# Four chained recurrent layers on one core: second gate computed with the state as the stationary operand, and the update gate's first half moved

## The chip, the cores and the metric

The kernel runs on one core of a Trainium2 chip. The metric is the device time of one launch in microseconds (us). TensorE (PE) multiplies, and its weight loads (PEld) overlap its matmuls; VectorE (DVE), ScalarE (ACT) and GpSimd (POOL) do the elementwise work; SyncE (SP) issues most of the transfers.

## The reference

Everything is float32, with B = 32 sequences of T = 256 steps of D = 256 features. Four layers follow each other, each added to its input:

```python
def step0(h, t):                      # layer 0, h starts at zero
    z = sigmoid(x[t] @ W_z + h @ U_z + cond @ C_z + b_z)      # update gate
    r = sigmoid(x[t] @ W_r + h @ U_r + cond @ C_r + b_r)      # reset gate
    hh = tanh(x[t] @ W + (r * h) @ U + cond @ C + b)          # candidate
    return (1 - z) * h + z * hh
x1 = x + scan(step0)
def step1(h, t):                      # layer 1, h starts at cond
    gate = sigmoid(h @ Wh.T + x1[t] @ Wz.T + b)               # the "second gate"
    return tanh(h * (1 - alpha) + gate * x1[t])
x2 = x1 + scan(step1)
x3 = x2 + linear_recurrence(x2)       # layer 2: gates, two scans over T
out = x3 + adapter(x3, cond)          # layer 3: two products with gelu and rank-8 terms
```

The change concerns `step0` and `step1` only.

## The kernel before

**Stages.** A loop runs the two recurrences together: at step t of layer 0 it does step t - 3 of layer 1 (`LAG` = 3). After it come 16 groups of two sequences each for layers 2 and 3. Every engine has its own instruction list, written out by hand; semaphores order the engines among each other. An engine executes its list in order. TensorE's loop holds four steps to a turn (`even`, `odd`, `even`, `odd`), the loops of the other engines hold sixteen.

**Layouts.** "Features on the partitions": a state is [128, 2, 32], each half of 128 features with 32 sequences along the free axis. "By rows": four slabs of 32 partitions, in each the 32 sequences on the partitions and 64 features along the free axis. `quarter` makes 4 matmuls with a 128x32 weight block stationary and the state's 32 columns moving; its output has features on the partitions. `by_rows` makes 4 matmuls per half with the state (128x32) stationary and 64 weight columns moving; its output is by rows, and a 32x32-block transpose on VectorE turns it back. The profile has two matmul records and two weight-load records for each matmul, as the operands are float32.

**A step on TensorE.** `first_gates`: the reset gate's four quarters `reset(k, m)` (k is the half of the state that is read, m the half of the output) and the update gate's two halves `update(k)` by rows. Then `ahead_first`, input products for steps to come, which need only x; `first_cand`, four quarters on `rh_f`; `second_gate`, four quarters on `h1_f`; and at the end `second_inputs` (two steps of `x1_f` times `wz1`, every other step) or `ahead_update`. That is 24 + 16 + 16 + 16 + 16 = 88 matmuls. Waits: `reset(0, 0)` for the first half of the new state (`h_done` 1), `reset(1, 0)` for the second (`h_done` 2), `first_cand` for the two halves of `rh_f`, `second_gate` for `h1_done`.

**A step on ScalarE.** Two reset sigmoids (L391), the update sigmoid `z_rows` (L396), the tanh of layer 1 `h1_f` (L413), two candidate tanhs (L402), the second gate's sigmoid `gate_f` (L408), then copies that seed PSUM banks with constants (L361, L364, L368).

**A step on VectorE.** Two products `rh_f` (L602), the transpose of `z_rows` (L607), `x1_f` of the step before (L632), `cand_kept` = (z - 1) h (L612), two scans that make the two halves of the new state (L622); then layer 1: `gx_f` = gate x1 (L638) and for each half `h1_pre` = h1 keep1 + gx (L644, `keep1` read as a scalar per partition).

**GpSimd** adds `x2` = x1 + h1 (L288), one instruction a step, once the second gate's product is done (`gate_pre`, since that shows that `h1_f` of the step is complete).

Of the kernel before, what the change touches and what calls it, by code (L numbers as in the profile page):

```python
# [11 lines left out]
B, T, D, R = 32, 256, 256, 8  # L12
P = 128
HALVES, SLABS, BLK = 2, 4, 32
SLAB = D // SLABS
SLOT = 8
BODY = 2 * SLOT
STEPS = 2
LAG = STEPS + 1
# [11 lines left out]
def build_program(nc, io):  # L31
# [3 lines left out]
    with ctx:  # L35
        def sb(name, shape, dt=fp32):
            return ctx.enter_context(nc.sbuf_tensor(name, shape, dt))
# [4 lines left out]
        def sem(name):  # L42
            return ctx.enter_context(nc.semaphore(name))
# [13 lines left out]
        seed_z = sb("seed_z", [P, STEPS, SLAB])  # L57
        seed_g = sb("seed_g", [P, HALVES, STEPS, B])

# [8 lines left out]
        none_h = sb("none_h", [P, 2, HALVES, B, 2])  # L68
        x1_f = sb("x1_f", [P, LOOP, HALVES, B])
        gate_f = sb("gate_f", [P, HALVES, B])  # L70
        keep1 = sb("keep1", [P, HALVES, B])
        h1_f = sb("h1_f", [P, 2, HALVES, B])
        gx_f = sb("gx_f", [P, HALVES, B])
        h1_pre = sb("h1_pre", [P, 2, HALVES, B])
        x2 = sb("x2", [P, HALVES, B, T])
# [58 lines left out]
        pre_z = [rows_of(banks[4 + n]) for n in range(2)]  # L134
        pre_g = [half(banks[6 + n]) for n in range(2)]
        pre_const = banks[7][:, 128:256].rearrange("p (a m b) -> p a m b", a=2, m=HALVES)
# [21 lines left out]
            sem("zero_done"), sem("rh_done"), sem("kept_done"), sem("h_done"), sem("x1_done"))  # L158
        gx_done, pre1_done, x2_done = (
            sem("gx_done"), sem("pre1_done"), sem("x2_done"))  # L160

# [184 lines left out]
        def _(act):  # L346
# [20 lines left out]
            def seed_gate(par):  # L367
                act.activation(flat(pre_g[par]), flat(seed_g[:]), ACT.Copy).then_inc(seeded, 1)  # L368

# [35 lines left out]
            def second_gate(n, u):  # L405
                t, s = n * BODY + u, u - LAG
                act.wait_ge(gate_pre, t + 1)
                act.activation(gate_f[:], pre_g[(s // STEPS) % 2][:, :, s % STEPS, :], ACT.Sigmoid).then_inc(gate_done, 1)  # L408

# [131 lines left out]
        def _(dve):  # L541
# [14 lines left out]
            def repeated(out, *parts):  # L556
                return [bass.broadcast_tensor_aps(out, part)[1] for part in parts]

            for m in range(HALVES):
                dve.tensor_copy(seed_g[:, m], *repeated(seed_g[:, m], bias_f[:, 3, m:m + 1])).then_inc(seeds_ready, 1)  # L560
            dve.wait_ge(first_in, 16 * len(FIRST_LOADS))
# [73 lines left out]
            def second_gated(n, u):  # L635
                s = n * BODY + u - LAG
                dve.wait_ge(gate_done, s + 1)
                dve.tensor_tensor(gx_f[:], gate_f[:], x1_f[:, (u - LAG) % LOOP], ALU.mult).then_inc(gx_done, 1)  # L638

            def second_sum(n, u):  # L640
                s, at = n * BODY + u - LAG, (u - LAG) % 2
                dve.wait_ge(gx_done, s + 1)
                for m in range(HALVES):
                    new = dve.scalar_tensor_tensor(h1_pre[:, at, m], h1_f[:, 1 - at, m], keep1[:, m, 0:1], gx_f[:, m],  # L644
                                                   ALU.mult, ALU.add)
                new.then_inc(pre1_done, 1)

# [90 lines left out]
        def _(pe):  # L738
# [41 lines left out]
            def ahead_second(at, par):  # L780

                for m in range(HALVES):
                    mm = ahead(pre_g[par][:, m].rearrange("p v b -> p (v b)"), m, col(wz1),
                               lambda k: x1_f[:, at:at + STEPS, k, :])
                return mm
# [46 lines left out]
            def first_gates(u):  # L832
                par, v, now = u // STEPS, u % STEPS, (u + 1) % 2
                state = lambda k: none_h[:, now, k, :, 1]
                reset = lambda k, m, **kw: quarter(pre_rh[par][m][:, 0, v, :], w_r, state, k, m, **kw)
                update = lambda k: by_rows(pre_z[par][:, v, :], state, lambda k, j: urz[:, k, j, 1, :], (k,))
                pe.wait_ge(h_done, 1)
                reset(0, 0)
                update(0)
                pe.wait_ge(h_done, 2)  # L840
                reset(1, 0, taken=h_done).then_inc(r_pre, 1)
                reset(0, 1)
                reset(1, 1).then_inc(r_pre, 1)
                update(1).then_inc(z_pre, 1)

            def second_gate(u, sums=None):
                s = u - LAG
                gate = lambda k, m: quarter(pre_g[(s // STEPS) % 2][:, m, s % STEPS, :], col(wh1),
                                            lambda k: h1_f[:, (s - 1) % 2, k], k, m)
                pe.wait_ge(h1_done, 1)  # L850
                if sums:
                    pe.wait_ge(pre1_done, sums)
                gate(0, 0).then_inc(h1_done, -1)
                gate(0, 1)
                gate(1, 0)
                gate(1, 1).then_inc(gate_pre, 1)

# [260 lines left out]
```

## Time and profile before

| | |
|---|---|
| median of 3 runs | 979.05 us (978.9 to 980.17) |
| profiled execution | 979.33 us, span 977.5 us |
| the loop of both recurrences | up to about 602 us |
| layers 2 and 3 | the rest |
| busy share PE / PEld / DVE / ACT / POOL | 96 / 79 / 87 / 62 / 22 % |

The span is the time from the first to the last instruction of the profiled execution. Rows of the timeline give the start in us from the span's start, the duration in us, engine, line, output and inputs, and how many instructions are merged in the row (x). Idle time is in brackets with what ended it.

### The profile page before, as it was taken

The page shows a single profiled execution, that of the slowest core. Times are in us where ns is not written, and L with a number is a line of the kernel's source. Part 1 is how long each engine was busy: PE and PEld are TensorE (multiplying, and loading weights), DVE is VectorE, ACT ScalarE, POOL GpSimd, SP SyncE. Part 2 cuts the span into 40 slices and gives each one's busy share as a digit, 9 for nine tenths or more (in the row PEclk, how much of TensorE's full clock was granted, in tenths as well). Part 3 has the DMA queues.
Part 4 walks back from the last instruction along what each step waited for, and adds up shares of the span by engine and source line. Part 5 has one row for each costly group of instructions (what it writes and reads, how often), then busy time and mean ns, then how long its engine had stood idle before and what let it go on. Part 6 is the DMA issues. An engine that isn't in the chain of part 4 may idle for free.

```text
span 977.5 us, 104703 instructions
## 1 busy us (share of the span) xinstructions
PE 938.2 (96%) x46862; PEld 768.3 (79%) x46862; DVE 850.6 (87%) x2882; ACT 601.4 (62%) x2607; POOL 216.7 (22%) x430
## 2 busy tenths in 40 slices
PE   6799999999999999999999999969999999999996
PEld 6799999999999999999999997335555555555554
DVE  3588888888888888888888887799999999999993
ACT  3577767767777777777777775335455556555552
POOL 0011111111111111111111111324334334433340
PEclk7999999999999999999999999979999999999999
DMA  5031330330100101001001000100010000001001
GB/s 178 24 99 50 121 112 24 123 111 24 38 24 24 38 24 35 27 27 35 27 24 38 24 27 9 28 0 26 24 41 32 24 24 24 24 24 47 25 25 43
DMA packets 38006, 41.48 MB, mean 42 GB/s; under 512 B 5088, under 2 KB 31200, under 8 KB 36832
## 3 DMA queue, kind: packets, MB, share of 16 engines
q1 hardware_dynamic: 36832, 40.55, 13.2%
q10 hardware_dynamic: 1152, 0.66, 0.2%
q8 instruction: 11, 0.18, 0.1%
q14 instruction: 11, 0.09, 0.0%
HBM read 32.28 MB, written 8.91 MB: 42 GB/s over the span
## 4 chain that ended last, share of the span: by engine, by line
PE 61%; DVE 29%; issue 7%; DMA 2%; ACT 1%; ACTq 0%; DVEq 0%
PE bank L826 26%; PE bank L757 18%; PE bank L772 13%; DVE arena L690 11%; DVE early L709 4%; DVE early L700 4%; DVE early L713 2%; DVE early L707 2%; DVE early L688 2%; DVE early L694 2%; DMA x_ahead<-in_x 1%; PE bank L934 1%; DMA beta<-in_beta 1%; PE bank L905 1%; PE bank L951 1%
## 5 line engine op out<-in xcount | busy, mean ns | idle before, releaser
L288 POOL TENSOR_TENSOR x<-x_f,h_f 128x64 f32 x256 | 84.1, 329 | 524.9 <-PE bank L826 523.8
L934 PE MATMUL bank<-x,wl 128*128 (+1 forms) x384 | 181.3, 611 | 0.9 <-DVE rank_rows L667 0.9
L757 PE MATMUL bank<-x_ahead,early 128*32 128x64 f32 x8256 | 173.6, 221 | 3.1 <-ACT bank L361 2.2
L772 PE MATMUL bank<-early,none_h 128*32 128x64 f32 x4096 | 167.3, 223 | 3.0 <-issue 3.0
L402 ACT ACTIVATE cand_kept<-bank 128x32 f32<-128x32 f32 x512 | 99.4, 203 | 92.3 <-PE bank L826 92.3
L826 PE MATMUL bank<-none_h,early 128*32 128x32 f32 x8192 | 150.3, 196 | 3.3
L622 DVE TENSOR_TENSOR_SCAN none_h<-zero_z,cand_kept 128x64 f32<-128x64 f32 x512 | 122.6, 282 | 30.7 <-ACT cand_kept L402 3.3
L757 PEld LDWEIGHTS bank<-x_ahead,early 128*32 128x32 f32 x8256 | 142.1, 110 | 4.0 <-issue 2.3
L826 PE MATMUL bank<-h_f,early 128*32 128x32 f32 x8288 | 140.5, 203 | 4.0 <-issue 3.0
L826 PEld LDWEIGHTS bank<-none_h,early 128*32 128x32 f32 x8192 | 131.3, 111 | 13.1 <-DVE none_h L622 12.9
L826 PE MATMUL bank<-rh_f,early 128*32 128x32 f32 x8192 | 140.5, 201 | 0.9 <-issue 0.5
L934 PEld LDWEIGHTS bank<-x,wl 128*128 128x128 f32 x384 | 68.8, 191 | 88.4 <-issue 88.4
L826 PEld LDWEIGHTS bank<-h_f,early 128*32 128x32 f32 x8288 | 118.5, 110 | 5.4 <-issue 3.6
L391 ACT ACTIVATE r_f<-bank 128x32 f32<-128x32 f32 x512 | 91.2, 197 | 48.1 <-PE bank L826 29.0
L826 PEld LDWEIGHTS bank<-rh_f,early 128*32 128x32 f32 x8192 | 112.6, 111 | 3.0 <-issue 0.6
L644 DVE SCALAR_TENSOR_TENSOR h_pre<-h_f,keep,gx_f 128x32 f32<-128x32 f32 x512 | 106.3, 249 | 9.1
L456 ACT ACTIVATE arena<-bank,bl 128x512 f32<-128x512 f32 x96 | 65.9, 687 | 76.9 <-PE bank L934 76.7
L602 DVE TENSOR_TENSOR rh_f<-r_f,none_h 128x32 f32<-128x32 f32 x512 | 89.0, 192 | 23.4 <-ACT r_f L391 23.3
L690 DVE RECIPROCAL arena<-early 128x512 f32<-128x512 f32 x32 | 107.3, 3353 | 1.1
L772 PEld LDWEIGHTS bank<-early,none_h 128*32 128x32 f32 x4096 | 103.9, 112 | 3.4 <-issue 3.4
L757 PE MATMUL bank<-x_f,early 128*32 128x64 f32 x4128 | 89.1, 223 | 1.2 <-issue 1.2
L772 PE MATMUL bank<-early,x_ahead 128*32 128x64 f32 x4128 | 88.4, 222 | 0.0
(103 smaller groups left out, 1528.1 us busy)
## 6 DMA issues: line engine op xcount, KB each, us to landing
x_ahead<-in_x SPq DMA_DIRECT2D x130, 64.0 KB, 1.8
x_in<-in_x SPq DMA_DIRECT2D x32, 256.0 KB, 2.6
arena<-in_w SPq DMA_DIRECT2D x8, 1024.0 KB, 6.8
out<-y SPq DMA_DIRECT2D x32, 256.0 KB, 2.4
rank_rows<-in_bias_rows SPq DMA_DIRECT2D x1, 1024.0 KB, 6.7
arena<-scratch SPq DMA_DIRECT2D x64, 16.0 KB
early<-in_cx SPq DMA_DIRECT2D x1, 768.0 KB, 4.4
early<-in_wx SPq DMA_DIRECT2D x1, 768.0 KB, 6.5
```

Source lines behind the costliest of these rows:

```text
L288: pool.tensor_tensor(x2[:, :, :, s], x1_f[:, u % LOOP], h1_f[:, u % 2], ALU.add).then_inc(x2_done, 1)
L391: act.activation(r_f[:, m], pre_rh[par][m][:, 0, v, :], ACT.Sigmoid).then_inc(r_done, 1)
L402: act.activation(cand_kept[:, u % 2, m, :, 0], pre_rh[par][m][:, 1, v, :], ACT.Tanh, scale=-1.0).then_inc(cand_done, 1)
L456: act.activation(dst[:, unit], banks[(at + 2 * par) % 4][:], fun, bias=bl2[:, mat, unit:unit + 1]).then_inc(done, 1)
L602: dve.tensor_tensor(rh_f[:, m], r_f[:, m], none_h[:, now, m, :, 1], ALU.mult).then_inc(rh_done, 1)
L622: dve.tensor_tensor_scan(pairs(none_h, m), pairs(zero_z, m), pairs(cand_kept, m), 0.0, ALU.mult, ALU.subtract).then_inc(h_done, 1)
L644: new = dve.scalar_tensor_tensor(h1_pre[:, at, m], h1_f[:, 1 - at, m], keep1[:, m, 0:1], gx_f[:, m], ALU.mult, ALU.add)
L690: dve.reciprocal(rec[:, k], s_t).then_inc(rec_done, 1)
L757: mm = pe.matmul(out[32 * j:32 * j + 32], weights(k, j, m), moving(k), start=False, stop=False, tile_position=(0, 32 * j), skip_group_chec ...
L772: mm = pe.matmul(out[32 * j:32 * j + 32], moving(k), weights(k, j), start=False, stop=False, tile_position=(0, 32 * j), skip_group_check=True)
L826: mm = pe.matmul(out[32 * j:32 * j + 32], weights(k, j, m), moving(k), start=False, stop=k == 1, tile_position=(0, 32 * j), skip_group_che ...
L934: mm = pe.matmul(banks[(at + 2 * par) % 4][:], wl2[:, k, mat, unit], x2[:, k, bass.ds(p * GB, GB), :].rearrange("p q t -> p (q t)"), start ...
```

## The change

The second gate's product takes the same form as the update gate's. `h1_f` becomes the stationary operand and 64 columns of `wh1` move, so 8 matmuls take the place of 16; its input products (`ahead_second`) keep their number of 16 and also swap operands. The sigmoid then writes `gate_rows`, by rows, and VectorE transposes that into `gate_f`. `h1 * keep1` becomes an instruction of its own (`kept1_f`), placed between the transpose and `gx_f`, and a single addition takes the place of the two fused multiply-adds. A wait on the transpose (`gate_turned`) stands ahead of `gx_f`. In `first_gates`, `update(0)` moves from behind `reset(0, 0)` to behind `reset(1, 1)`.

```diff
             def second_gate(n, u):
-                act.activation(gate_f[:], pre_g[(s // STEPS) % 2][:, :, s % STEPS, :], ACT.Sigmoid).then_inc(gate_done, 1)
+                act.activation(gate_rows[:, s % 2], pre_g[(s // STEPS) % 2][:, s % STEPS], ACT.Sigmoid).then_inc(gate_done, 1)
...
             def second_gated(n, u):
                 dve.wait_ge(gate_done, s + 1)
+                dve.transpose(gate_f[:].rearrange("p m b -> p (m b)"), gate_rows[:, (u - LAG) % 2]
+                              ).then_inc(gate_turned, 1)
+                dve.tensor_tensor(kept1_f[:], h1_f[:, (u - LAG + 1) % 2], keep1[:], ALU.mult).then_inc(gx_done, 1)
+                dve.wait_ge(gate_turned, s + 1)
                 dve.tensor_tensor(gx_f[:], gate_f[:], x1_f[:, (u - LAG) % LOOP], ALU.mult).then_inc(gx_done, 1)
             def second_sum(n, u):
-                dve.wait_ge(gx_done, s + 1)
-                for m in range(HALVES):
-                    new = dve.scalar_tensor_tensor(h1_pre[:, at, m], h1_f[:, 1 - at, m], keep1[:, m, 0:1], gx_f[:, m],
-                                                   ALU.mult, ALU.add)
-                new.then_inc(pre1_done, 1)
+                dve.wait_ge(gx_done, 2 * (s + 1))
+                dve.tensor_tensor(h1_pre[:, at], kept1_f[:], gx_f[:], ALU.add).then_inc(pre1_done, 1)
...
             def ahead_second(at, par):
-                for m in range(HALVES):
-                    mm = ahead(pre_g[par][:, m].rearrange("p v b -> p (v b)"), m, col(wz1),
-                               lambda k: x1_f[:, at:at + STEPS, k, :])
+                for v in range(STEPS):
+                    mm = by_rows(pre_g[par][:, v, :], lambda k: x1_f[:, at + v, k, :], lambda k, j: wz1[:, k, j, :])
...
                 pe.wait_ge(h_done, 1)
                 reset(0, 0)
-                update(0)
                 pe.wait_ge(h_done, 2)
                 reset(1, 0, taken=h_done).then_inc(r_pre, 1)
                 reset(0, 1)
                 reset(1, 1).then_inc(r_pre, 1)
+                update(0)
                 update(1).then_inc(z_pre, 1)
             def second_gate(u, sums=None):
-                gate = lambda k, m: quarter(pre_g[(s // STEPS) % 2][:, m, s % STEPS, :], col(wh1),
-                                            lambda k: h1_f[:, (s - 1) % 2, k], k, m)
+                gate = lambda k: by_rows(pre_g[(s // STEPS) % 2][:, s % STEPS, :], lambda k: h1_f[:, (s - 1) % 2, k],
+                                         lambda k, j: wh1[:, k, j, :], (k,))
                 pe.wait_ge(h1_done, 1)
-                gate(0, 0).then_inc(h1_done, -1)
-                gate(0, 1)
-                gate(1, 0)
-                gate(1, 1).then_inc(gate_pre, 1)
+                gate(0).then_inc(h1_done, -1)
+                gate(1).then_inc(gate_pre, 1)
```

The seed of the second gate's banks (`seed_g`) is laid out by rows as well; its copies keep their sizes.

## Rows read from the trace of the kernel before

**Rows 1.** The page: chain that ended last, by engine; one group of instructions.

```profile
PE 61%; DVE 29%; issue 7%; DMA 2%; ACT 1%; ACTq 0%; DVEq 0%
...
L602 DVE TENSOR_TENSOR rh_f<-r_f,none_h 128x32 f32<-128x32 f32 x512 | 89.0, 192 | 23.4 <-ACT r_f L391 23.3
```

**Rows 2.** Windows, 200 to 500 us: busy time (instructions) by engine, PEclk, DMA share, GB/s.

```profile
200.00:500.00 300.00, 297.77 (x23509) 291.16 (x23501) 265.63 (x1337) 214.34 (x1204) 44.03 (x134) 1.00 0.13 36
```

**Rows 3.** The scans that make the state (L622), whole kernel.

```profile
L622 DVE TENSOR_TENSOR_SCAN none_h<-zero_z,cand_kept x512: 264/291/296, 18.3 to 601.7; 128x64 f32<-128x64 f32 x171
```

**Rows 4.** Timeline of one step, its reset gate to its new state.

```profile
304.03 0.18 PEld L826 LDWEIGHTS bank<-none_h,early 128*32 128x32 f32 x6
304.08 0.24 PE L826 MATMUL bank<-none_h,early 128*32 128x32 f32 x6
...
304.57 0.22 PE L772 MATMUL bank<-early,none_h 128*32 128x64 f32 x1
304.59 0.65 PE L757 MATMUL bank<-x_ahead,early 128*32 128x64 f32 x31
304.60 0.36 ACT L391 ACTIVATE r_f<-bank 128x32 f32<-128x32 f32 x2
304.83 0.35 DVE L602 TENSOR_TENSOR rh_f<-r_f,none_h 128x32 f32<-128x32 f32 x2
304.86 0.22 ACT L396 ACTIVATE z_rows<-bank 128x64 f32<-128x64 f32 x1
304.98 0.25 ACT L413 ACTIVATE h_f<-h_pre 128x64 f32<-128x64 f32 x1
305.08 0.44 PEld L826 LDWEIGHTS bank<-rh_f,early 128*32 128x32 f32 x32
305.08 0.55 PE L826 MATMUL bank<-rh_f,early 128*32 128x32 f32 x32
305.11 0.25 DVE L607 STREAM_TRANSPOSE zero_z<-z_rows 128x64 f32<-128x64 f32 x1
305.28 0.18 DVE L632 TENSOR_TENSOR x_f<-x_in,none_h 128x64 f32<-128x64 f32 x1
305.42 0.46 PEld L826 LDWEIGHTS bank<-h_f,early 128*32 128x32 f32 x32
305.45 0.52 PE L826 MATMUL bank<-h_f,early 128*32 128x32 f32 x31
305.47 0.23 DVE L612 SCALAR_TENSOR_TENSOR cand_kept<-zero_z,none_h 128x64 f32<-128x64 f32 x1
305.57 0.39 ACT L402 ACTIVATE cand_kept<-bank 128x32 f32<-128x32 f32 x2 [0.35 <-PE bank L826]
305.80 0.66 PE L772 MATMUL bank<-early,x_ahead 128*32 128x64 f32 x31
305.81 0.47 DVE L622 TENSOR_TENSOR_SCAN none_h<-zero_z,cand_kept 128x64 f32<-128x64 f32 x2
```

**Rows 5.** Timeline, layer 1 and the state's scans one step earlier.

```profile
303.64 0.47 DVE L622 TENSOR_TENSOR_SCAN none_h<-zero_z,cand_kept 128x64 f32<-128x64 f32 x2
303.91 0.23 ACT L408 ACTIVATE gate_f<-bank 128x64 f32<-128x64 f32 x1
304.05 0.33 POOL L288 TENSOR_TENSOR x<-x_f,h_f 128x64 f32 x1 [1.84 <-PE bank L826]
304.17 0.28 DVE L638 TENSOR_TENSOR gx_f<-gate_f,x_f 128x64 f32<-128x64 f32 x1
304.49 0.41 DVE L644 SCALAR_TENSOR_TENSOR h_pre<-h_f,keep,gx_f 128x32 f32<-128x32 f32 x2
```

**Rows 6.** Timeline at TensorE's back edge, and the scans after it.

```profile
306.51 0.16 PEld L826 LDWEIGHTS bank<-none_h,early 128*32 128x32 f32 x7 [0.21 <-DVE none_h L622]
...
308.26 0.48 DVE L622 TENSOR_TENSOR_SCAN none_h<-zero_z,cand_kept 128x64 f32<-128x64 f32 x2
```

**Rows 7.** L638 and L288 from 30 to 600 us: durations min/median/max in ns.

```profile
L638 DVE TENSOR_TENSOR gx_f<-gate_f,x_f x252: 224/284/370, 35.5 to 599.8; 128x64 f32<-128x64 f32 x126
...
L288 POOL TENSOR_TENSOR x<-x_f,h_f x251: 322/329/335, 37.9 to 599.7; 128x64 f32 x126
```

**Rows 8.** Timeline in the setup: two VectorE products, the second waiting for the first.

```profile
12.78 0.22 DVE L586 TENSOR_TENSOR scaled<-normed,gamma 128x64 f32<-128x64 f32 x1
13.04 0.22 DVE L588 TENSOR_TENSOR ada<-scaled,beta 128x64 f32<-128x64 f32 x1
```

**Rows 9.** A scan of the later stage (L700) that at times meets GpSimd work.

```profile
L700 DVE TENSOR_TENSOR_SCAN early<-early,first_one x32: 1214/1216/2292, 628.8 to 955.2; 128x514 f32<-128x514 f32 x32
```

More of the change, by code:

```diff
@@ L57, in build_program @@
         seed_z = sb("seed_z", [P, STEPS, SLAB])
-        seed_g = sb("seed_g", [P, HALVES, STEPS, B])
+        seed_g = sb("seed_g", [P, STEPS, SLAB])
         x_in = sb("x_in", [P, 2, SLOT, HALVES, B])
@@ L69, in build_program @@
         x1_f = sb("x1_f", [P, LOOP, HALVES, B])
+        gate_rows = sb("gate_rows", [P, 2, SLAB])
         gate_f = sb("gate_f", [P, HALVES, B])
@@ L73, in build_program @@
         gx_f = sb("gx_f", [P, HALVES, B])
+        kept1_f = sb("kept1_f", [P, HALVES, B])
         h1_pre = sb("h1_pre", [P, 2, HALVES, B])
@@ L134, in build_program @@
         pre_z = [rows_of(banks[4 + n]) for n in range(2)]
-        pre_g = [half(banks[6 + n]) for n in range(2)]
+        pre_g = [rows_of(banks[6 + n]) for n in range(2)]
         pre_const = banks[7][:, 128:256].rearrange("p (a m b) -> p a m b", a=2, m=HALVES)
@@ L158, in build_program @@
             sem("zero_done"), sem("rh_done"), sem("kept_done"), sem("h_done"), sem("x1_done"))
-        gx_done, pre1_done, x2_done = (
-            sem("gx_done"), sem("pre1_done"), sem("x2_done"))
+        gate_turned, gx_done, pre1_done, x2_done = (
+            sem("gate_turned"), sem("gx_done"), sem("pre1_done"), sem("x2_done"))
         ln_step, std_done, ada_done, hid_pre, hid_done = (
@@ L367, in seed_gate @@
             def seed_gate(par):
-                act.activation(flat(pre_g[par]), flat(seed_g[:]), ACT.Copy).then_inc(seeded, 1)
+                act.activation(pre_g[par].rearrange("p v e -> p (v e)"), seed_g[:].rearrange("p v e -> p (v e)"),
+                               ACT.Copy).then_inc(seeded, 1)
             act.wait_ge(table_in, 1)
@@ L557, in repeated @@
                 return [bass.broadcast_tensor_aps(out, part)[1] for part in parts]
-            for m in range(HALVES):
-                dve.tensor_copy(seed_g[:, m], *repeated(seed_g[:, m], bias_f[:, 3, m:m + 1])).then_inc(seeds_ready, 1)
+            for v in range(STEPS):
+                dve.tensor_copy(seed_g[:, v], bias_rows[:, 3]).then_inc(seeds_ready, 1)
             dve.wait_ge(first_in, 16 * len(FIRST_LOADS))
@@ L780, in ahead_second @@
             def ahead_second(at, par):
-                for m in range(HALVES):
-                    mm = ahead(pre_g[par][:, m].rearrange("p v b -> p (v b)"), m, col(wz1),
-                               lambda k: x1_f[:, at:at + STEPS, k, :])
+                for v in range(STEPS):
+                    mm = by_rows(pre_g[par][:, v, :], lambda k: x1_f[:, at + v, k, :], lambda k, j: wz1[:, k, j, :])
                 return mm
```

## The prediction

> **What bounds the kernel now.** I read the page first: its chain that ended last lies on PE for 61% and on DVE for 29% [rows 1]. The windows then show the recurrent loop almost full on PE: 297.8 of 300 us busy, DVE 265.6, ACT 214.3, at a granted clock of 1.00, the 2.4 GHz level, so no clock is to be won [rows 2]. The last scan of the state starts at 601.7 us [rows 3]; only what lies ahead of it can change much.
>
> The timeline gives the loop's rhythm. From scan to scan a step takes 305.81 - 303.64 = 2.17 us, and the one that holds PE's back edge 308.26 - 305.81 = 2.45 [rows 4 to 6]. A turn of four is 3 x 2.17 + 2.45 = 8.96 us. PE's 23509 records in 300 us are 300/8.96 x 4 = 134 steps of 176, two for each of the 88 matmuls. 2.17 us over 88 matmuls is 24.7 ns each: in three steps of four PE is fed one matmul after another, with only short stalls. In the fourth, it pays about 0.28 us more for the branch, although the new state is there: the reset gate's first load comes at 306.51, while the scan pair had ended at 305.81 + 0.47 = 306.28 [rows 4, 6].
>
> PE is not alone. The loop's dependences nearly close in the same 2.17 us: reset gate, sigmoid, product, candidate, tanh, scan, back to the reset gate. The first half of the state is ready at about 303.64 + 0.29 + 0.05 = 303.98, PE starts on it at 304.03 [rows 3 to 5]. So any saving on PE beyond 0.05 us in those three steps runs into this chain, and what counts is how long the chain is after the change.
>
> **The change part by part.**
> *Second gate.* 16 matmuls of 32 columns become 8 of 64. Before, 31 records start within 0.52 - 0.20 = 0.32 us, some 0.34 for all 32 [rows 4]. A record of 64 columns takes (0.66 - 0.22)/30 = 14.7 ns [rows 4], so 16 take 0.23: 0.11 us less for each step. As a stream, 80 x 24.7 ns = 1.98 us, 0.2 below the old step. PE alone would then give 4 x 1.98 + 0.28 = 8.20 us a turn.
>
> *Input products of the second gate.* 16 matmuls with 64 moving columns before and after: nothing. The seed's copies keep their size: nothing, as ACT is idle for almost a third of the loop [rows 2].
>
> *The update gate moves back.* In the old order update(0) filled PE's time while the second scan ran. Now PE waits there after reset(0, 0), and 8 records x 14.7 ns = 0.12 us more stand between the second half of the state and z_pre. The reset gate gains: both r_pre signals come earlier by up to that 0.12. The new chain through the update gate, from the end of the scan pair:
> PE sees it 0.05 later (a product of L602, 192 ns, starts at 304.83, and PE's load at 305.08 [rows 1, 4]); then 24 records of 32 columns and 16 of 64. The old mixed stretch gives 0.49 us for 48 records (304.08 to 304.57 [rows 4]), 10.2 ns each, so 0.41 for 40; fed at the old pace of 12.35 ns a record it would be 0.49. I take 0.43, since PE has just stood still and has its instructions queued. Last update record to sigmoid 304.86 - 304.57 = 0.29. Sigmoid to transpose 305.11 - 304.86 = 0.25. Transpose to L632 0.17, L632 to L612 0.19, L612 itself 0.23 [rows 4]; then the wait for it, about 0.06 (a DVE product that waits for its predecessor starts 13.04 - 12.78 - 0.22 = 0.04 after its end [rows 8], and a second wait stands here); the scan pair 0.47. Sum 0.05 + 0.43 + 0.29 + 0.25 + 0.17 + 0.19 + 0.23 + 0.06 + 0.47 = 2.14 us (2.12 to 2.20). By the other branch (reset gate, tanh) it is shorter by about 0.07, since in the old step tanh and not L612 released the scan and now r_pre is earlier. So the update gate becomes the chain that sets the step, just below the old 2.17.
>
> *VectorE, layer 1.* Old: L638 to L644 0.32, L644 to the next L602 0.34, together 0.66 us of the list [rows 4, 5]. New: transpose to kept1 0.17 (as L607 to L632), the transpose's 0.25 and 0.03 of waiting put gx at 0.28; gx lasts 0.22 alone and 0.28 beside GpSimd [rows 7]; 0.04 later the addition, whose successor starts some 0.14 behind it: 0.28 + 0.28 + 0.04 + 0.14 = 0.74. That is 0.08 more. But the sigmoid comes 0.11 earlier, and the transpose can begin right at the end of the scans, where gx stood 0.06 behind it. So rh_f could start 0.68 to 0.74 after the scan pair, while the reset chain asks for it at 0.05 + 0.07 (8 records) + 0.26 + 0.23 = 0.61, the second half at 0.80. DVE makes the first half late by up to 0.1, which the 0.07 that this branch is ahead, and the later second half, roughly cover. Behind the new wait (gate_turned) stand gx, the addition and then rh_f of the next step, so this is where DVE would become the bound.
>
> *h1's tanh (L413)* sits in ACT's list behind the update sigmoid, 0.12 later, and takes 0.25 [rows 4]. z_pre being late, h1_f is ready 0.05 + 0.43 + 0.29 + 0.12 + 0.25 + 0.05 = 1.19 after the scans. PE reaches the second gate 0.34 after its candidate load, which comes 0.25 after rh_f: 0.61 + 0.25 + 0.34 = 1.20. Just hidden.
>
> *Back edge.* PE is done with its fill at about 0.05 + 0.43 + 0.46 + 0.34 + 0.23 + 0.46 = 1.97 after the scans. With 0.28 of branch and 0.08 of reset(0, 0) it is ready for the second half of the state at 2.33 in the worst case, 0.14 behind 2.14 + 0.05; if the branch runs ahead of a queue that is now fuller, nothing is lost. I take 0.05.
>
> *Sum.* A turn is 4 x 2.14 + 0.05 = 8.61 us against 8.96, 0.35 less. There are 64 turns; the first two wait for weights, 62 count: 21.7 us. The three layer 1 steps behind the loop get perhaps 0.5 us longer together. 979.33 - 21.7 + 0.5 = 958.1 us; the median of the runs is 0.28 below the profiled execution, so 958.
>
> **Rivals.**
> *PE stays fed at the old pace behind the scans, or pays the branch.* 0.49 for the update stretch gives 2.20, and with 0.1 to 0.15 of back edge 8.90 to 8.95; halfway, 8.78, it is 62 x 0.18 = 11 us less: 968. For it: the records do run at 12.35 ns on average. Against: after a stall they ran at 10.
>
> *GpSimd's addition meets the scans: slower.* Each L638 beside L288 lasts longer than the 224 ns it needs alone, and ends 0.07 after it (304.17 + 0.28 against 304.05 + 0.33) [rows 5, 7]; a scan of L700 has taken 2292 ns for 1216 [rows 9]. L288 follows gate_pre, which comes 0.11 earlier against the candidate, while the scans come 0.07 later against it. It now starts 304.05 - 303.64 = 0.41 behind the first scan, and would then start 0.41 - 0.18 = 0.23 behind it, at the moment of the second scan (0.2). If it gets in first, the scan pair ends at 0.23 + 0.33 + 0.07 = 0.63 in place of 0.47: 2.14 + 0.16 = 2.30 a step, 9.20 a turn, 62 x 0.24 = 15 us more: 994. It decides once L288 starts before the second scan. Against it: a start just behind makes GpSimd wait instead, and costs only a longer kept1 or gx. The Trainium skill (SBUF — State Buffer, "SBUF: two separate sides") calls the pair of ports that both engines share an exclusive lock, held for the whole instruction by whichever starts first, against a DVE instruction with two SBUF inputs. The L638 rows agree with that; by the rule a scan behind L288 would be held for all of it, the same 994.
>
> *VectorE becomes the bound.* If kept1 and gx are both stretched beside GpSimd, 0.1 to 0.15 more, a turn is 4 x 2.27 = 9.08: 987.
>
> *The update gate eats all of it.* Each saving goes into the later z_rows, 2.20 a step and 0.15 of branch: 8.95, no change, 979.
>
> *The update gate is not last.* The shorter reset branch sets 2.07, a turn 8.28 to 8.3: 62 x 0.67 = 41 us less, 938.
>
> **Chances.** Forecast 0.56, the old pace 0.18, the scan met by GpSimd 0.09, VectorE 0.05, no change 0.06, update gate not last 0.06. Two in a thousand, 2 us, is about what a measurement of this kernel tells from no change. Faster 0.80, within 0.06, slower 0.14. The range 946 to 981 us leaves out the two slower cases and most of the last one, 0.2; that of the forecast alone is 950 to 966.
>
> **What would show it.** The gap between L622 pairs about even at 2.1 to 2.2 in all four steps; PE idle ahead of the reset gate, released by L622; L622 released by L612 and not by L402; PE at some 160 records a step; L638 down to 190 to 224 ns. Wrong if L622 is longer than 0.3 us beside L288, if L602 waits on its own engine rather than on L391, or if the fourth step stays at 2.4.

## The result and the profile after

The changed kernel takes 968.98 us (median of four runs, 968.64 to 970.43) against 978.97 us for the kernel before (978.52 to 980.17): a ratio of 0.990, 95% interval 0.988 to 0.992, or 10 us less. The forecast was 958 us. The direction holds and the time lies inside the range, but the gain is less than half of the 21 us foretold. The profiled execution took 969.18 us, its span 967.4; the profiled one of before had 977.5. One run of the experiments below, of the kernel with the old order, came out slow at 980.86 us with a granted clock of 0.94 against 0.98 to 0.99 in its others, and its ratio leaves that run out.

The budget comes first. I cut both spans at two scans of the state: that of the eighth step, and the last one. Windows of the kernel before (its last one begins with the last step's scans and holds all that follows them), then of the kernel after; the first number of a row is the length, then busy time by engine, granted clock, DMA share and GB/s:

```profile
core 0: us, PE busy (x) PEld busy (x) DVE busy (x) ACT busy (x) POOL busy (x), PEclk, DMA share, GB/s
0.00:43.97 43.97, 31.08 (x1584) 28.75 (x1584) 18.03 (x93) 17.84 (x80) 3.19 (x11) 0.84 0.30 105
43.97:601.49 557.52, 553.40 (x43666) 541.26 (x43658) 493.37 (x2481) 397.78 (x2233) 81.51 (x248) 1.00 0.16 48
601.49:977.50 376.01, 353.74 (x1648) 198.28 (x1638) 339.19 (x309) 185.76 (x296) 132.04 (x171) 0.98 0.08 27
```

```profile
0.00:40.58 40.58, 30.24 (x1470) 27.79 (x1474) 18.31 (x98) 18.06 (x80) 3.30 (x11) 0.87 0.32 113
40.58:588.76 548.18, 541.65 (x39696) 509.96 (x39688) 501.82 (x2728) 413.58 (x2233) 93.59 (x248) 1.00 0.15 49
588.76:967.40 378.64, 354.20 (x1584) 198.47 (x1572) 337.56 (x313) 185.78 (x296) 132.01 (x171) 0.98 0.08 27
```

The 62 turns become 9.3 us shorter (557.5 to 548.2, or 8.99 to 8.84 us a turn), the start 3.4 us shorter, and what stands behind the last scan 2.6 us longer: 9.3 + 3.4 - 2.6 = 10.1 us, the whole difference of the spans. The granted clock in the loop is 1.00 in both. PE has 43666 - 39696 = 3970 records fewer there, as it should (8 matmuls, 16 records, in each of 248 steps are 3968), and now idles 6.5 us in place of 4.1.

An ordinary step, in the timeline of the kernel after (start, length, engine, line; in brackets the idle time and what ended it). It answers to [rows 4, 5]:

```profile
304.08 0.47 DVE L625 TENSOR_TENSOR_SCAN none_h<-zero_z,cand_kept 128x64 f32<-128x64 f32 x2
...
304.29 0.39 POOL L290 TENSOR_TENSOR x<-x_f,h_f 128x64 f32 x1 [1.77 <-PE bank L776]
304.42 0.47 PEld L829 LDWEIGHTS bank<-none_h,early 128*32 128x32 f32 x32
...
304.47 0.22 DVE L641 STREAM_TRANSPOSE gate_f<-gate_rows 128x64 f32<-128x64 f32 x1
304.61 0.18 DVE L643 TENSOR_TENSOR kept_f<-h_f,keep 128x64 f32<-128x64 f32 x1
304.72 0.23 DVE L645 TENSOR_TENSOR gx_f<-gate_f,x_f 128x64 f32<-128x64 f32 x1
...
304.97 0.36 ACT L394 ACTIVATE r_f<-bank 128x32 f32<-128x32 f32 x2 [0.22 <-PE bank L829]
304.98 0.22 DVE L650 TENSOR_TENSOR h_pre<-kept_f,gx_f 128x64 f32<-128x64 f32 x1
...
305.20 0.35 DVE L605 TENSOR_TENSOR rh_f<-r_f,none_h 128x32 f32<-128x32 f32 x2
305.30 0.22 ACT L399 ACTIVATE z_rows<-bank 128x64 f32<-128x64 f32 x1
...
305.56 0.25 DVE L610 STREAM_TRANSPOSE zero_z<-z_rows 128x64 f32<-128x64 f32 x1
305.72 0.18 DVE L635 TENSOR_TENSOR x_f<-x_in,none_h 128x64 f32<-128x64 f32 x1
...
305.91 0.23 DVE L615 SCALAR_TENSOR_TENSOR cand_kept<-zero_z,none_h 128x64 f32<-128x64 f32 x1
305.94 0.39 ACT L405 ACTIVATE cand_kept<-bank 128x32 f32<-128x32 f32 x2 [0.28 <-PE bank L829]
...
306.25 0.47 DVE L625 TENSOR_TENSOR_SCAN none_h<-zero_z,cand_kept 128x64 f32<-128x64 f32 x2
```

From scan to scan it is 306.25 - 304.08 = 2.17 us, as long as the step of [rows 4]; the median of such steps is 2.158. Follow the update gate: scans end 304.55, sigmoid 305.30, transpose 305.56, L635 305.72, L615 305.91 to 306.14, scan 306.25. PE has stood still at `PEld L829`: eight loads of reset(0, 0) at 304.42 to 304.47, then nothing until 304.60. That is the new wait for the second half of the state.

The fourth step, which holds PE's back edge, answers to [rows 6]:

```profile
332.69 0.47 DVE L625 TENSOR_TENSOR_SCAN none_h<-zero_z,cand_kept 128x64 f32<-128x64 f32 x2
...
333.20 0.50 PEld L829 LDWEIGHTS bank<-none_h,early 128*32 128x32 f32 x32 [0.23 <-DVE none_h L625]
...
333.72 0.36 ACT L394 ACTIVATE r_f<-bank 128x32 f32<-128x32 f32 x2 [0.36 <-PE bank L829]
...
334.09 0.22 ACT L399 ACTIVATE z_rows<-bank 128x64 f32<-128x64 f32 x1
...
335.03 0.63 DVE L625 TENSOR_TENSOR_SCAN none_h<-zero_z,cand_kept 128x64 f32<-128x64 f32 x2
335.20 0.32 POOL L290 TENSOR_TENSOR x<-x_f,h_f 128x64 f32 x1 [1.91 <-PE bank L776]
```

It lasts 335.03 - 332.69 = 2.34 us. The branch ends just in time: PE loads from 333.20, 0.04 after the scans' end at 333.16. But all 32 loads of the reset gate, reset(0, 0) too, stand behind that moment. Their first 15 start within 0.11 us, and then none starts for 0.16 us. The update sigmoid comes 334.09 - 333.16 = 0.93 after the scans in place of 305.30 - 304.55 = 0.75: 0.18 late, and the step is 0.17 longer. Over the loop such a stop right behind the 15th load (over 0.06 us from one load to the next) shows in 52 of 60 turns, mostly 0.10 us long. The four places of a turn within VectorE's loop of 16 steps give 2.27, 2.28, 2.34 and 2.38 us (medians; the last holds VectorE's own branch).

The scan pair at the end of that fence is 0.63 long and not 0.47. GpSimd's addition started at 335.20, before the second scan. Of the 252 second scans that run beside layer 1, 15 last 0.42 to 0.43 us and one 0.35, where all others last 0.264 to 0.272, and in each of the 16 the addition starts at least 0.038 us ahead of the scan. Where it starts less far ahead, the scan is undisturbed and the addition is the one that lasts longer, 0.38 to 0.42 in place of 0.33. The groups of both, one line and all its instructions (min/median/max ns):

```profile
L625 DVE TENSOR_TENSOR_SCAN none_h<-zero_z,cand_kept x492: 264/290/430, 42.9 to 584.7; 128x64 f32<-128x64 f32 x164
```

```profile
L290 POOL TENSOR_TENSOR x<-x_f,h_f x246: 323/385/424, 43.1 to 584.7; 128x64 f32 x123
```

The last part is behind the loop. PE's timeline of the kernel after, from the last scans on:

```profile
588.57 0.63 PE L776 MATMUL bank<-early,x_ahead 128*32 128x64 f32 x32
590.23 0.42 PE L776 MATMUL bank<-early,h_f 128*32 128x64 f32 x12 [1.03 <-ACT h_f L416]
593.48 0.25 PE L776 MATMUL bank<-early,h_f 128*32 128x64 f32 x2 [2.83 <-issue]
```

The kernel before waits 0.94 us for the tanh there too, and has one stop for nothing that the profile shows, a short one in the products that follow the gate:

```profile
606.54 0.63 PE L905 MATMUL bank<-arena,hid_f 128*32 128x512 f32 x3 [0.86 <-issue]
```

In the kernel after, PE stops for 2.83 us in the middle of a second gate, again waiting for nothing that the profile shows. The three steps of layer 1 that are left over follow one another, so each is late by it: their sigmoids come 5.07, 9.15 and 11.19 us after the last scan, where before they came at 2.16, 6.48 and 8.49.

### The profile page after: what moved, and what is told of

The parts are those of the page before. It is cut to its first block, busy times and chain, and to the rows that moved or that the text cites. A ratio compares the mean times of both kernels' runs of the same rounds, so it can differ in the third digit from the quotient of the medians.

```text
span 967.4 us, 96701 instructions
## 1 busy us (share of the span) xinstructions
PE 926.1 (96%) x42718; PEld 736.2 (76%) x42718; DVE 857.7 (89%) x3138; ACT 617.4 (64%) x2607; POOL 228.9 (24%) x430
## 4 chain that ended last, share of the span: by engine, by line
PE 47%; DVE 39%; issue 10%; ACT 2%; DMA 1%; DVEq 1%; ACTq 0%
PE bank L829 18%; PE bank L776 18%; DVE arena L694 11%; PE bank L761 8%; DVE early L713 4%; DVE early L704 4%; DVE none_h L625 3%; DVE early L717 2%; DVE early L711 2%; DVE early L692 2%; DVE zero_z L610 2%; DVE early L698 2%; DVE cand_kept L615 2%; ACT z_rows L399 1%; PE bank L935 1%
## 5 line engine op out<-in xcount | busy, mean ns | idle before, releaser
L290 POOL TENSOR_TENSOR x<-x_f,h_f 128x64 f32 x256 | 96.4, 377 | 502.7 <-PE bank L776 501.6
L829 PE MATMUL bank<-none_h,early 128*32 128x32 f32 x8192 | 149.8, 201 | 6.6 <-DVE none_h L625 0.4
L829 PEld LDWEIGHTS bank<-none_h,early 128*32 128x32 f32 x8192 | 113.8, 110 | 37.6 <-DVE none_h L625 17.9
L829 PE MATMUL bank<-rh_f,early 128*32 128x32 f32 x8192 | 129.0, 199 | 2.2 <-issue 1.6
L829 PEld LDWEIGHTS bank<-rh_f,early 128*32 128x32 f32 x8192 | 111.7, 111 | 3.6 <-issue 1.7
L776 PE MATMUL bank<-early,none_h 128*32 128x64 f32 x4096 | 110.0, 221 | 1.6 <-issue 1.6
L776 PE MATMUL bank<-early,h_f 128*32 128x64 f32 x4144 | 107.8, 220 | 3.9 <-issue 2.8
L605 DVE TENSOR_TENSOR rh_f<-r_f,none_h 128x32 f32<-128x32 f32 x512 | 89.6, 193 | 13.6 <-ACT r_f L394 9.8
L776 PE MATMUL bank<-early,x_f 128*32 128x64 f32 x4128 | 83.1, 220 | 0.0
L776 PE MATMUL bank<-early,x_ahead 128*32 128x64 f32 x4128 | 81.8, 220 | 0.0
L776 PEld LDWEIGHTS bank<-early,h_f 128*32 128x32 f32 x4144 | 73.2, 111 | 5.9 <-issue 3.9
L776 PEld LDWEIGHTS bank<-early,none_h 128*32 128x32 f32 x4096 | 75.8, 111 | 1.8 <-issue 1.8
L776 PEld LDWEIGHTS bank<-early,x_f 128*32 128x32 f32 x4128 | 68.1, 110 | 0.2
```

The lines of the kernel that those rows point to most:

```text
L290: pool.tensor_tensor(x2[:, :, :, s], x1_f[:, u % LOOP], h1_f[:, u % 2], ALU.add).then_inc(x2_done, 1)
L605: dve.tensor_tensor(rh_f[:, m], r_f[:, m], none_h[:, now, m, :, 1], ALU.mult).then_inc(rh_done, 1)
L776: mm = pe.matmul(out[32 * j:32 * j + 32], moving(k), weights(k, j), start=False, stop=False, tile_position=(0, 32 * j), skip_group_check=True)
L829: mm = pe.matmul(out[32 * j:32 * j + 32], weights(k, j, m), moving(k), start=False, stop=k == 1, tile_position=(0, 32 * j), skip_group_che ...
```

## The experiments

The theories, by the letters of the expectations. **A**: the update gate's chain, lengthened by update(0) behind the whole reset gate, sets the step. **B**: VectorE's longer list for the second gate sets it. **C**: the reset gate's branch sets it. **D**: the stop behind the loop comes from where the loop's end lies in PE's program, not from the second gate's form. **F**: this stop and the one at the back edge come and go with the halves of a block of that program. **E** and **G** are told where they are tested. Each group of runs was timed beside the kernel before on the same chip.

**The old order, in the new kernel.**

```diff
                 reset(0, 0)
+                update(0)
                 pe.wait_ge(h_done, 2)
                 reset(1, 0, taken=h_done).then_inc(r_pre, 1)
                 reset(0, 1)
                 reset(1, 1).then_inc(r_pre, 1)
-                update(0)
                 update(1).then_inc(z_pre, 1)
```

> The changed kernel with update(0) put back between reset(0, 0) and the wait for the second half of the state; the turned second gate stays. Theory A (the update gate, made late by the move, sets the step: 2.16 us from scan to scan, released by cand_kept): z_rows comes 0.11 us earlier against the scans, the reset gate's branch then sets 2.05 to 2.10, a turn of four 8.35 to 8.5 in place of 8.84, and the kernel takes 943 to 952 us. Theory B (VectorE's longer list, or the pace at which TensorE is fed, sets the step): no change, 967 to 971. Theory C (the reset gate is last and the move brought the gain): 975 or more.

966.84 us, ratio 0.988 (0.986 to 0.989). Its timeline:

```profile
300.31 0.48 DVE L625 TENSOR_TENSOR_SCAN none_h<-zero_z,cand_kept 128x64 f32<-128x64 f32 x2
...
301.45 0.22 ACT L399 ACTIVATE z_rows<-bank 128x64 f32<-128x64 f32 x1
...
302.06 0.23 DVE L615 SCALAR_TENSOR_TENSOR cand_kept<-zero_z,none_h 128x64 f32<-128x64 f32 x1
...
302.41 0.29 DVE L625 TENSOR_TENSOR_SCAN none_h<-zero_z,cand_kept 128x64 f32<-128x64 f32 x1
```

The sigmoid comes 301.45 - 300.79 = 0.66 after the scans and not 0.75, and the step is 2.10 us. So for three steps of four A is right: the late update(0) costs 0.06. But the fourth steps grow to 2.35, 2.36, 2.49 and 2.41, and the turn is 8.75, not 8.4: of 11.7 us that the other steps gain over the loop, the fourth ones give back 6.2, and the 943 to 952 us expected are missed. By the two ratios, the new kernel's order costs some 2 us in all against the old one, and their intervals overlap.

**The new order, in the kernel before** (the same two lines moved the other way).

> The kernel before with only update(0) moved behind the reset gate. Theory A: TensorE's 88 matmuls at 24.7 ns set 2.17 us before, the update chain of 2.16 lies just below, so 979 plus or minus 3, rather above. Theory C (the reset gate is last): 3 to 10 us faster, 969 to 976.

978.74 us, ratio 0.999 (0.998 to 1.001); steps of 2.168 and 2.47, a turn of 8.98. As A has it, there is nothing to win by the order alone, and C falls: with the reset gate last, this edit should have taken 3 to 10 us off. The gain of the change comes from the second gate's form.

**The leak fused again, in the new kernel.** VectorE's product is left out and two fused operations take the place of the addition.

```diff
-                dve.tensor_tensor(kept1_f[:], h1_f[:, (u - LAG + 1) % 2], keep1[:], ALU.mult).then_inc(gx_done, 1)
...
-                dve.wait_ge(gx_done, 2 * (s + 1))
-                dve.tensor_tensor(h1_pre[:, at], kept1_f[:], gx_f[:], ALU.add).then_inc(pre1_done, 1)
+                dve.wait_ge(gx_done, s + 1)
+                for m in range(HALVES):
+                    new = dve.scalar_tensor_tensor(h1_pre[:, at, m], h1_f[:, 1 - at, m], keep1[:, m, 0:1], gx_f[:, m],
+                                                   ALU.mult, ALU.add)
+                new.then_inc(pre1_done, 1)
```

> The changed kernel with the leak product back in the two fused instructions, behind the transpose and gx. rh_f of the next step can start 0.12 us later than now, its second half 0.06 later; the tanh branch has 0.07 us in hand at the scan. Theory A: 968 to 972. Theory B (VectorE sets the step): 0.1 us a step, 62 turns of four, 25 us more, 990 to 998.

971.46 us, ratio 0.992 (0.991 to 0.994). The turn is 8.85 and the loop 548.8 us (548.2), so B falls: VectorE's list does not set the step. What follows the last scan takes 380.3 us against 378.6, but this can't be put down to the fused operations: the first experiment, which leaves them out, has 380.2.

**32 matmuls of zeros ahead of the loop.** They run at the start on banks that are being cleared anyway, and change no value; what they shift is where the loop and its end lie in PE's program.

```diff
-            for n in range(8):
+            for n in 5 * list(range(8)):
                 mm = pe.matmul(banks[n][:, 0:128], zeros[:, 0:P], zeros[:, 0:128], start=True, stop=True)
```

> The changed kernel with 32 more zero matmuls ahead of everything, on banks that are zeroed there anyway; they give back in TensorE's program the length that the loop lost. Theory D (the 2.6 us lost between the last scan and layer 2 are TensorE waiting for instructions, because the shorter loop moved a block border of its program from the adapter's matmuls into the second gate): 2 to 3 us less, 966 to 967.5, the second gate's sigmoid about 2.2 us after the last scan in place of 5.1. Rival (the wait comes from the new gate's own chain): 969 to 970.

966.17 us, ratio 0.987 (0.985 to 0.989). PE behind the loop:

```profile
590.16 0.43 PE L776 MATMUL bank<-early,h_f 128*32 128x64 f32 x16 [1.03 <-ACT h_f L416]
...
593.52 0.25 PE L776 MATMUL bank<-early,h_f 128*32 128x64 f32 x3 [0.56 <-issue]
```

The second gate is whole again, and of 2.83 us a stop of 0.56 is left, one gate later. The stop has moved by what was added: from the start of the last step's scans, 28 matmul records of PE stand ahead of it in the changed kernel and 91 here, 63 more, where 32 matmuls are 64 records (a trace can miss a few). What follows the last scan takes 375.7 us in place of 378.6: D is right. Two things were not expected. The start is 5 us longer, 45.6 us to the eighth step's scan: one more block of program arrives there (last section). And the loop is 5 us shorter, 543.1. Its fourth steps give 3.7 us of that: the stop behind the back edge is gone, in all of 60 turns. Besides, only 4 second scans are held by GpSimd and not 16; why, isn't shown. This kernel's loads of a reset gate right behind the branch, to set beside the 0.50 of 333.20:

```profile
334.88 0.35 PEld L829 LDWEIGHTS bank<-none_h,early 128*32 128x32 f32 x32 [0.23 <-DVE none_h L625]
```

The fourth steps are 2.21, 2.21, 2.24 and 2.38, where they were 2.27, 2.28, 2.34 and 2.38.

**16 in place of 32** (`3 * list(range(8))`).

> The changed kernel with 16 more zero matmuls ahead of everything in place of the 32 of e4_padded. In e4_padded the second short stop of TensorE behind its branch (0.10 us, 18 loads on) was gone and the fourth step took 2.21 in place of 2.28 to 2.34 us. Theory F (where the loop lies in the blocks of TensorE's program sets that stop, in halves of such a block): still there, or moved to another place in the step; the fourth step 2.25 to 2.35, in all 967 to 970. Rival (any more instructions ahead of the loop do it): 2.21 again, 965 to 967.

965.49 us, ratio 0.987 (0.984 to 0.990). The fourth steps are 2.205, 2.206, 2.234 and 2.384, and 374.1 us stand behind the last scan: half the shift does as much as the whole. No turn has the stop behind the branch, and the one behind the loop is gone too. F's rule for when the stops come therefore falls for the back edge, and its rival's number holds. Both runs show that matmuls added ahead of the loop take the stops away; the place of the loop in the program is what they have in common, but they also start the loop later, and which place is good isn't shown.

**GpSimd released one step later,** by the sigmoid's count instead of PE's, so that its addition falls elsewhere.

```diff
-                    pool.wait_ge(gate_pre, s + LAG + 2)
+                    pool.wait_ge(gate_done, s + 2)
...
-            pe.sem_inc(gate_pre, 1)
+            pe.sem_inc(gate_done, 1)
```

> The changed kernel with GpSimd's addition waiting for the second gate's sigmoid (gate_done) in place of its product (gate_pre). In the changed kernel 16 of 252 second scans last 0.42 to 0.43 us in place of 0.27, and these are the ones that GpSimd's addition precedes by 0.038 us or more. Theory E (the addition that gets in first holds the scan): no stretched second scan is left, 16 x 0.16 = 2.6 us less, 966 to 967. Rival (the addition then meets the leak product and gx, and VectorE becomes late): 969 to 975.

973.72 us, ratio 0.994 (0.993 to 0.996). Theory E, that the addition that gets in first holds the scan, wanted 966 to 967. No second scan is held any more, and the thirteenth step of 16, where most of them were, is 2.159 in place of 2.32: the addition was the cause. But the kernel is not faster, its ratio is even 0.004 above that of the changed one, and its rival's number, 969 to 975, holds. The profiled execution, the fastest of ten at 971.35 us, has a loop of 549.3 us: the fourth steps are 2.35, 2.29, 2.29 and 2.52 and take back more than the scans gave. Another 1.1 us come on behind the loop. Why the fourth steps grew isn't shown.

**Old order and 32 matmuls of zeros together.**

> e1_old_order with the 32 zero matmuls of e4_padded: update(0) in its old place, the turned second gate. In e1 three steps in four take 2.10 us, the fourth 2.35 to 2.53. Theory A with F: the stop behind the branch goes, the fourth step 2.25 to 2.3, a turn 8.57 to 8.62 in place of 8.75, and the wait behind the loop goes, the start is 3 to 4 us later: 958 to 962. Rival (the fourth step is set by the branch alone, whatever lies behind it): the turn stays at 8.75, 966 to 968.

962.76 us, ratio 0.984 (0.982 to 0.987). Steps 2.10, fourth steps 2.31, 2.31, 2.41 and 2.41, a turn of 8.71. The stop behind the branch is gone in all of 60 turns, where the old order alone has it in 27, and the one behind the loop is down from 2.72 to 0.21 us, 64 records further on. But the fourth steps do not come down to the 2.25 to 2.3 expected: the time lies just above A's and F's 958 to 962, the turn nearer to the rival's 8.75, and both are right in part.

**Update(0) late only in the step behind the branch.** In three steps it fills PE's wait, in the fourth PE has no wait to fill.

```diff
                 reset(0, 0)
+                if u:
+                    update(0)
...
                 reset(1, 1).then_inc(r_pre, 1)
-                update(0)
+                if not u:
+                    update(0)
```

> The changed kernel with update(0) moved back only in the step behind TensorE's branch (u = 0) and in its old place in the three others. Theory A (the update gate sets the three ordinary steps when it is late, 2.16 against 2.10 us in e1) and theory G (behind the branch TensorE's queue is empty and the reset gate sets that step, so there the late place is the better one: 2.27 to 2.34 against 2.35 to 2.53): a turn 3 x 2.10 + 2.3 = 8.60 to 8.65 in place of 8.84, 955 to 960 us. Rival (the time lost is only passed from one step to the next): a turn of 8.75 as in e1, 966 to 968.

965.36 us, ratio 0.984 (0.981 to 0.987), where 955 to 960 was hoped for. This is theory G: behind the branch the late place is the better one. The steps are 2.10 but the fourth 2.39, the turn 8.75 as in the first experiment, which is the rival's number. Its reason, a loss that is only passed on, is not quite what the traces have: over the loop the fourth steps are 1.4 us shorter than in the first experiment, and the others 1.2 us longer, as GpSimd holds 15 second scans here and 6 there.

**The same with 16 matmuls of zeros.**

> e8_late_once with 16 more zero matmuls ahead of everything, as in e6_padded_16. Theories A, G and F: the fourth step 2.2 to 2.25, a turn 8.52 to 8.6, 950 to 956 us. Rival: as e7_old_order_padded, 962 to 964.

959.77 us, ratio 0.980 (0.977 to 0.982). This is the best version, 9 us below the changed kernel and 19 below the one before, though its interval touches that of the old order with 32 matmuls. Steps 2.10, fourth steps 2.28, 2.29, 2.31 and 2.41, a turn of 8.68, and 8 second scans held. No turn has the stop behind the branch. Both numbers expected are missed, the 950 to 956 of the theories and the 962 to 964 of the rival: the fourth steps stay above 2.2 to 2.25.

**L615 ahead of L635.** In the update chain L615 starts 305.91 - 305.56 = 0.35 behind the transpose's start, with L635 in between. Here L635 goes behind it, and SP's wait for the input buffer goes one step later, because L635 reads that buffer.

```diff
-                sp.wait_ge(kept_done, 2 * (n * BODY + (s + 1) * SLOT + 1))
+                sp.wait_ge(kept_done, 2 * (n * BODY + (s + 1) * SLOT + 2))
...
                     update_turned(n, u)
+                    kept_state(n, u)
...
                         first_output(n, u - 1, first)
-                    kept_state(n, u)
                     next_state(n, u)
```

> The changed kernel with x1 (L635) behind cand_kept (L615) on VectorE, and SyncE's wait ahead of the load of x_in one step later, since x1 now reads x_in behind cand_kept. Theory A (transpose, x1, cand_kept lie in one row on the update gate's path, 0.36 us from the transpose to cand_kept): cand_kept starts 0.28 to 0.3 behind the transpose, the three ordinary steps 2.09 to 2.11, a turn 8.60 to 8.70, 955 to 963 us. Against it, x1 ends 0.2 later, and every other step TensorE wants it for the second gate's inputs: if that is what counts, 968 to 975. Theory B (VectorE's list or TensorE's pace): no change, 969.

1018.29 us, ratio 1.040 (1.039 to 1.042). L615 starts 0.351 behind the transpose's start in place of 0.353 (medians), with nothing between them: it waits for the transpose's result, and L635 costs the chain nothing. What the edit does cost is in the chain of waits between 220 and 580 us (us, times, longest):

```profile
PEld bank L761 <- DMA x_ahead<-in_x: 20.6, 9, 2.4
...
PEld bank L776 <- DVE x_f L635: 16.6, 65, 0.3
```

Every second step is 2.27, since PE waits for the first layer's output. And once in 16 steps there is one of 4.27 us: SP's queue stands at the later wait, so the transfer of `x_ahead` behind it is issued a whole step later, and that step is 2.1 us longer than the others. No expectation had this: the highest named was 975.

## Why the prediction was right in direction and wrong in size

**Update gate last: right.** Its chain in the ordinary step, from the end of the scans, measured against the sum of the prediction: PE 0.05 (0.05), 40 records 0.43 (0.43), sigmoid starts 0.27 later (0.29), 0.26 (0.25), 0.17 (0.17), 0.19 (0.19), 0.23 (0.23), wait 0.10 (0.06), scans 0.47 (0.47): 2.17 against 2.14. Only the wait between L615 and the scan was taken too short. The 0.17 and 0.19 through L632 (now L635) came out as a sum but name the wrong step: the last experiment has the same 0.35 without it, so this is the wait for the transpose. `gx_f` takes 223 to 227 ns between 200 and 500 us, alone now, near the 190 to 224 foretold. The other branch had 0.07 us in hand, as foretold: tanh's first half ended at 306.14 and would have let the scan go at about 306.18. The first two experiments show the rest.

**The step that failed is the turn, "4 x 2.14 + 0.05 = 8.61 us", above all its back edge of 0.05.** The turn measures 8.84. The three ordinary steps give 3 x 0.018 = 0.05 of the difference of 0.23. GpSimd's hold of a scan gives 0.16 / 4 = 0.04, since it strikes about one step in 16. The rest, 0.14, is the fourth step, 2.33 on the mean against 2.14 + 0.05. A fourth step is on the mean 0.17 longer than an ordinary one, just over the worst case of the prediction (0.14), which held the branch and the 8 records of reset(0, 0). The sum's old turn was also a little short, 8.96 from one step each, where the 62 turns measure 8.99: hence 62 x (0.23 - 0.03) = 12.4 us between the 21.7 forecast and the 9.3 measured. The branch itself does end in time, 0.04 behind the scans. The 8 records stand in the open, 8 x 10.7 ns = 0.09 us. And the loads behind the branch do not keep the pace that the prediction took for all steps because PE "has its instructions queued": they stop once more for 0.10 to 0.16 us. The kernels with added matmuls lose that stop, and with it 0.06 to 0.10 us of each fourth step but the last. Why added matmuls remove it is not settled. Of the signs that the prediction named for being wrong, one came, scans of 0.42 us beside GpSimd's addition, and its even gap in all four steps did not: the fourth are 2.27 to 2.38.

**Behind the loop: "perhaps 0.5 us longer" was 2.6.** The stop of 2.83 us is more than the whole of it: the first sigmoid left over comes 5.07 - 2.16 = 2.91 us later, the last one 2.70. And it has to do with where the code behind the loop lies in PE's program, not with the second gate's form: with that form kept and matmuls added the part is no longer than before the change (374.1 and 375.7 against 376.0). The kernel before was not run with added matmuls, so what they would do for its own stop of 0.86 isn't known.

**The start was left out:** 3.4 us came from it that the prediction did not have. The first turn is where PE's program arrives, and the shorter loop has one block less to wait for: five transfers of 16 KB in place of six (below). The added matmuls bring the sixth back, whatever their number: 32 made it 45.57 us to the eighth step's scan in place of 40.58, 16 made it 45.9, and in the best kernel 16 made it 43.7.

So the forecast's -21.7 + 0.5 became -9.3 + 2.6 - 3.4 = -10.1 us.

**The rivals.** "PE stays fed at the old pace, or pays the branch", 968, names the time almost to the microsecond, but by luck, and only its second half is true: the records ran at 10.7 ns, the turn is 8.84 and not 8.78, and the start and the end, which it leaves out or has at 0.5, happen to make up for it. The scan met by GpSimd is real at the price named, 0.16 us, though not from the point named: to start ahead of the second scan is not enough, it takes 0.038 us. It happens in 16 of 252 steps, so it is worth some 2.6 us in all and no 994. In the ordinary step GpSimd starts at 304.29, 0.21 behind the first scan (0.23 forecast), and the second scan at the same 304.29: the case was decided by a few hundredths. The rule of the Trainium skill (SBUF — State Buffer, "SBUF: two separate sides"), that whichever of the two engines starts first holds the port pair for its whole instruction, agrees with these rows in both directions, scans of 0.43 behind the addition and additions of 0.38 to 0.42 behind the scan, but for one strip: an addition that starts up to 0.037 us ahead still lets the scan through. VectorE as the bound falls by the third experiment; the reset branch as the last one falls by the second.

## What to carry to other kernels

When a saving makes a loop wait on its dependences, price the step behind the back edge by itself: what was done under the previous wait in other steps is done in the open there. A reordering is worth little by itself if one step in four gives back half of it; look for the step that didn't get shorter. And before believing a few microseconds in either direction, shift the loop in the program by some harmless instructions: here that alone was worth 3 us (ratios 0.987 and 0.990, whose intervals overlap a little), and together with the better order 9.

## What the runs showed of the hardware

Matmuls added ahead of the loop were worth at least as much as the order of its gates: by the medians 3 to 6 us against 0 to 3. The section on DMA queues of the page counts program as transfers of its own, here of the kernel after:

```profile
q8 instruction: 10, 0.16, 0.1%
```

That is 16 KB a transfer; the kernel before has 11. I take them for PE's program, since PE's stops go with them behind the loop, and its time at the start with their number.

At the start they follow each other by some 3.6 us (13.6, 17.2, 20.8, 24.4, 27.9 in the kernel after). The changed kernel and its variants without added matmuls have five of them there and reach the eighth step's scan at 39.9 to 40.6 us. The kernel before, its variant with the other order and the four kernels with added matmuls have six, and reach it at 43.7 to 45.9.

In the loop there are none, from 27.9 to 591.1 us, though its branch is taken in each turn. So, as far as these rows show, what the back edge costs is not the wait for such a transfer.

Behind the loop the first one starts 2.3 to 2.4 us after the last step's first scan in all but one of the kernels (2.8 with 16 matmuls added to the changed one). Wherever PE makes its stop for no reason shown behind the loop, it goes on 2.2 to 2.8 us after this transfer's start: at 593.48 after one at 591.1 in the changed kernel, at 593.52 after 591.1 with 32 matmuls added, at 606.54 after 603.8 in the kernel before. So how long PE stands still depends on how early it comes to the stop. In the changed kernel and its variants without added matmuls it comes there 1.9 to 2.1 us behind the last step's first scan and stands for 2.7 to 3.1; in the kernel before, its variant and the two with 32 matmuls added it comes there at 4.1 to 4.3 us and stands for 0.2 to 1.0. With 16 added there is no such stop.

The Trainium skill (Runtime: NRT & Kernel Launch, "Instruction fetch mechanics") has each engine's program arrive in blocks of 16 KiB or 256 instructions, ahead of use, with a taken branch breaking the sequence; the size agrees with the rows above. That the block is late only because the loop's branch had kept the fetch back is my reading of it, and no run here shows the mechanism itself.

GpSimd's hold of a scan is nearly all or nothing, and about 0.001 us decides it: in the kernel with update(0) late only once and 16 matmuls of zeros, of two additions that start 0.039 us ahead of the second scan one leaves it at 0.264 us and the other holds it to 0.425; all that start earlier hold it, and all that start later do not.
